# Block attention on row and column tiles: score tiles in pairs, three value buffers, later copies and normalising

## The reference

```python
B, S, D, H = 16, 128, 128, 16          # as called here; a head has D / H = 8 features
q, k, v = split_heads(x @ Wq), split_heads(x @ Wk), split_heads(x @ Wv)
scores = jnp.einsum('bhqd,bhkd->bhqk', q, k) / jnp.sqrt(jnp.float32(HD))
attn_w = jax.nn.softmax(scores, axis=-1)
ctx = jnp.einsum('bhqk,bhkd->bhqd', attn_w, v)
attn_out = ctx.transpose(0, 2, 1, 3).reshape(b, s, d) @ Wo + bo
out1 = _layernorm(x + attn_out, ln1_g, ln1_b)
# then: router on out1, 8 experts, second layernorm
```

## Time and profile before

| | |
|---|---|
| median of 3 runs | 1589.41 us (1586.63 to 1589.45) |
| the profiled execution's own time | 1589.34 us |
| its span, first to last instruction | 1587.6 us |
| outside the span | 1.7 us |
| busy in the span: PE, PEld, DVE, ACT, POOL | 87%, 68%, 53%, 46%, 9% |
| the block attention stage | 1130.1 to 1314.9 us, 184.8 us |
| mean granted TensorE clock | 0.924 of 2.4 GHz |

### The profile page before, as it was taken

One profiled execution on the slowest core, in us unless ns is written; L12 is line 12 of the kernel. 1 busy time (PEld: TensorE's weight loads), 2 busy tenths in 40 slices (PEclk: granted clock), 3 DMA queues, 4 the chain that ended last, 5 costly groups with the idle time before them and its releaser, 6 DMA issues. The chain is left out here.

```text
span 1587.6 us, 27487 instructions
## 1 busy us (share of the span) xinstructions
PE 1382.5 (87%) x9061; PEld 1082.9 (68%) x9061; DVE 839.1 (53%) x2258; ACT 728.7 (46%) x1657; POOL 147.1 (9%) x256
## 2 busy tenths in 40 slices
PE   6765799999996799789999997984699996999995
PEld 5642477777775387579999986973477773666764
DVE  4549676677662554635555543447677762122224
ACT  4331677777762402245555552442355542333333
POOL 1010000000001000000000002005244421000000
PEclk9869899999996999879999997995699996999998
DMA  8000000000000000000000004002000000000000
GB/s 330 1 1 0 1 1 1 2 1 1 1 1 1 1 1 0 1 1 2 1 1 1 1 2 105 16 1 106 0 1 1 0 1 1 1 1 1 0 1 27
DMA packets 6429, 24.55 MB, mean 15 GB/s; under 512 B 797, under 2 KB 1311, under 8 KB 5418
## 3 DMA queue, kind: packets, MB, share of 16 engines
q1 hardware_dynamic: 6314, 23.03, 4.2%
HBM read 21.98 MB, written 1.05 MB: 15 GB/s over the span
## 5 line engine op out<-in xcount | busy, mean ns | idle before, releaser
L1306 DVE SCALAR_TENSOR_TENSOR XN<-bank,gate,XN 128x128 f32<-128x128 f32 x256 | 89.8, 351 | 224.7 <-PE bank L1270 222.2
L1286 ACT ACTIVATE e_hidden<-bank,small 128x512 f32<-128x512 f32 x152 | 104.4, 687 | 214.5 <-PE bank L1258 214.4
L766 PE MATMUL bank<-a_va,a_pT 128*128 128x65 f32 x1024 | 130.3, 270 | 0.7 <-ACT a_pT L933 0.6
L1011 DVE TENSOR_REDUCE a_mx<-bank 128x4 f32<-128x512 f32 x128 | 87.9, 686 | 80.0 <-PE bank L806 79.7
L1270 PEld LDWEIGHTS bank<-attention_weights,e_hidden 128*128 128x128 f32 x1024 | 119.2, 192 | 14.8 <-issue 14.8
L766 PEld LDWEIGHTS bank<-a_va,a_pT 128*128 128x128 f32 x1024 | 125.2, 193 | 2.5 <-ACT a_pT L933 1.1
L1258 PE MATMUL bank<-XNT,attention_weights 128*128 128x512 f32 x256 | 121.2, 606 | 1.2 <-PEq L541 1.2
L1270 PE MATMUL bank<-attention_weights,e_hidden 128*128 128x128 f32 x1024 | 119.3, 275 | 0.0
L831 PE MATMUL bank<-attention_weights,a_cv 128*128 128x256 f32 x256 | 84.4, 411 | 15.0 <-issue 15.0
L933 ACT ACTIVATE a_pT<-bank 128x512 f32<-128x512 f32 x128 | 76.1, 595 | 41.9 <-PE bank L840 39.2
L1019 DVE TENSOR_TENSOR a_shifted<-bank,a_mx 128x512 f32<-128x512 f32 x128 | 88.3, 690 | 3.4
(11 more groups left out here) (351 smaller groups left out, 2709.9 us busy)
## 6 DMA issues: line engine op xcount, KB each, us to landing
attention_weights<-in_a SPq DMA_DIRECT2D x2, 2048.0 KB, 11.8
mod_ring<-in_mod_weights SPq DMA_DIRECT2D x4, 576.0 KB
ctx_both<-in_ctx SPq DMA_DIRECT2D x1, 2048.0 KB, 9.5
attention_weights<-in_up SPq DMA_DIRECT2D x1, 2048.0 KB, 7.7
attention_weights<-in_down SPq DMA_DIRECT2D x1, 2048.0 KB, 13.7
down<-in_down SPq DMA_DIRECT2D x1, 1536.0 KB, 18.3
down<-in_mod_weights SPq DMA_DIRECT2D x2, 576.0 KB
X<-in_x SPq DMA_DIRECT2D x4, 256.0 KB, 3.9
```

Of the source, the lines that this page charges most:

```text
L766: last = pe.matmul(value_bank[:, j * (W + 1):(j + 1) * (W + 1)], pT[:, i.slot(2), j * 128:(j + 1) * 128], va[:, p, g // 2 * 8 + 2 * j + g ...
L1011: dve.tensor_reduce(mx[:, i.slot(2), :], score_bank[i.slot(2)][:, :].rearrange("p (h s) -> p h s", h=4), AX.X, ALU.max).then_inc(maxed, 1)
L1286: act.activation(hidden[0:rows, p, f, :], up_bank_of(i, f)[0:rows, :], function, bias=up_bias(g, f)).then_inc(hidden_ready, 1)
L1306: dve.scalar_tensor_tensor(out=total, in0=down_bank[j][:, e * D:(e + 1) * D], scalar=gate_column(k, 4 * q + j, g * per_group + e), in1=tot ...
```

## The change

**Scores on row tiles.** The projected q and k lie with 4 heads in each group of 32 rows. `kD` shrinks from 16 masked copies of k to 4: copy j keeps in every group of 32 rows the rows of that group's head j (mask `own`, made once on DVE). The scores of group r are a matmul over rows 32r to 32r+31 alone, and the matmuls of two groups follow each other in different row tiles of the array and different banks. There are four score banks in place of two. POOL makes `kD` with one instruction a batch in place of four.

**Values on column tiles.** The roles are swapped: a window of 32 columns of `va` is the weight, the transposed probabilities (128 columns) move, and the result appears already transposed, 32 partitions a group of four heads. A head's 8 features stand in `va` every 40 columns with zeros between, so that a window at 32j past a group's start holds head j at its own place and zeros elsewhere; four matmuls accumulate in a column tile. A second set of 16 matmuls with a weight of ones gives every row its sum. All 32 of a batch are issued together, once `pT` of all four items is kept (`pT` now holds 2 batches of 4 items), and three buffers of `va` take turns. The turn of the result and ACT's copy of it fall away, and DVE's reciprocal covers 128 columns.

**The probabilities' turn** is now an ordinary matmul with the identity as the moving side.

**Later steps.** ACT's copy of `pT` gets a lag of its own, 6. Lags change from NORM_O 6, OUT 7, ADD 7, NORMALISE 8, KEEP 9, TURN_OUT 10 to NORM_O 8, OUT 8, ADD 9, NORMALISE 10, AFFINE 11, KEEP 15, TURN_OUT 15. Scale and shift of the output and its copy go from DVE to POOL (AFFINE). The output's bank half moves: `y_bank` shares the values' bank, the turned output the projection's. PE's order within a step becomes project, values, turn P, score, out, turn out. All sweeps of the stage are written out without a loop.

```diff
-    PROJECT, KEEP_QKV, BLOCKS, SCORE, EXP, TURN_P, VALUES, NORM_O, TURN_O, OUT, ADD, NORMALISE, KEEP, TURN_OUT = \
-        0, 1, 4, 3, 5, 5, 6, 6, 7, 7, 7, 8, 9, 10
+    PROJECT, KEEP_QKV, BLOCKS, SCORE, EXP, TURN_P, KEEP_P, VALUES, NORM_O, OUT, ADD, NORMALISE, AFFINE, KEEP, TURN_OUT = \
+        0, 1, 2, 3, 5, 5, 6, 6, 8, 8, 9, 10, 11, 15, 15
...
+        score_bank, turn_bank, value_bank, project_bank = k.ps[0:4], k.ps[4:6], k.ps[6], k.ps[7]
+        turned_out, y_bank = project_bank[:, 384:512], value_bank[:, 256:384]
...
-            pool.memset(va[:, :, :, W:W + 1], 1.0).then_inc(cleared, 1)
+            pool.memset(va[:, :, :], 0.0).then_inc(cleared, 1)
+            pool.memset(ones[:, :], 0.0).then_inc(cleared, 1)
+            pool.wait_ge(cleared, 2)
+            pool.memset(ones[:, :].rearrange("p (j w) -> p j w", w=40)[:, :, 0:W], 1.0).then_inc(cleared, 1)
...
+                i = at(VALUES)
                 if i.alive and i.offset % 4 == 3:
+                    n, p = b.number, b.slot(2)
+                    await_count(pe, p_kept, 4 * n + 4)
                     if b.older_than(1):
+                        await_count(pe, o_normed, n)
+                        await_count(pe, added, n)
...
+                    for at_column, stationary, per_group in ((0, va[:, n % 3, :], 160), (S, ones[:, :], 0)):
+                        for j in range(4):
+                            for c in range(4):
+                                first = c * per_group + 32 * j
+                                last = pe.matmul(value_bank[32 * c:32 * c + 32, at_column:at_column + S],
+                                                 stationary[:, first:first + 32], pT[:, p, c, j * 128:(j + 1) * 128],
+                                                 start=j == 0, stop=j == 3, tile_position=(0, 32 * c))
...
-                        last = pe.transpose(turn_bank[p][:, j * 128:(j + 1) * 128],
-                                            probs[:, p, j * 128:(j + 1) * 128], k.ident)
+                        last = pe.matmul(turn_bank[p][:, j * 128:(j + 1) * 128],
+                                         probs[:, p, j * 128:(j + 1) * 128], k.ident, start=True, stop=True)
...
+                i = at(SCORE)
+                if i.alive and i.offset % 2 == 0:
+                    await_count(pe, k_spread, b + 1)
+                    if i.older_than(4):
+                        await_count(pe, subtracted, m - 2)
+                    for r in (g, g + 1):
+                        rows = slice(32 * r, 32 * r + 32)
+                        pe.matmul(score_bank[r][:, :], qT[rows, p, :],
+                                  kD[rows, p, :, :].rearrange("p h s -> p (h s)"), start=True,
+                                  stop=True).then_inc(scored, 1)
...
+                i = at(NORM_O)
                 if i.alive and i.offset % 4 == 3:
...
+                    dve.reciprocal(rec[:, :], value_bank[:, S:2 * S]).then_inc(inverted, 1)
...
+                    dve.tensor_tensor(oT[:, :], value_bank[:, 0:S], rec[:, :], ALU.mult).then_inc(o_normed, 1)
...
                 i = at(SCORE)
                 if i.alive:
-                    await_count(dve, scored, m + 1)
+                    await_count(dve, scored, m + 2 - i.offset % 2)
                     dve.tensor_reduce(mx[:, p, :], bank, AX.X, ALU.max).then_inc(maxed, 1)
```

More of the change, by code:

```diff
@@ L1843, in body @@
                 i = at(BLOCKS)
[L1844 to L1852, removed]
+                if i.alive and i.offset % 4 == 0:
+                    b = batch_of(i)
+                    n, p = b.number, b.slot(2)
+                    await_count(pool, qkv_kept, n + 1)
+                    if b.older_than(2):
+                        await_count(pool, scored, 4 * n - 4)
+                    elif n == 0:
+                        pool.wait_ge(own_ready, 1)
+                    pool.tensor_tensor(kD[:, p, :, :], kT[:, p, :].unsqueeze(1).to_broadcast([128, 4, S]),
+                                       own[:, :].unsqueeze(2).to_broadcast([128, 4, S]), ALU.mult).then_inc(k_spread, 1)
+                i = at(AFFINE)
+                if i.alive and i.offset % 4 == 3:
+                    b = batch_of(i)
+                    n, p = b.number, b.slot(2)
+                    await_count(pool, scaled_ready, n + 1)
+                    if b.older_than(2):
+                        await_count(pool, out_turned, n - 1)
+                        await_count(pool, copied, n - 1)
+                    pool.tensor_tensor(out[:, p, :], scaled[:, p, :], k.affine3(2), ALU.mult).then_inc(chain, 1)
+                    await_count(pool, chain, n + 1)
+                    pool.tensor_tensor(out[:, p, :], out[:, p, :], k.affine3(3), ALU.add).then_inc(out_ready, 1)
+                    await_count(pool, out_ready, n + 1)
+                    pool.tensor_copy(col(k.out1, n), out[:, p, :]).then_inc(copied, 1)
+            sweep(pool, G, 8, TURN_OUT, body, rolled=False)
         @block.tensor
@@ L1859, in body @@
             def body(at):
[L1860 to L1864, removed]
                 i = at(PROJECT)
@@ L1875, in body @@
                               stop=True).then_inc(projected, 1)
[L1876 to L1884, removed]
@@ L1916, in body @@
                     b = batch_of(i)
-                    await_count(pe, o_kept, b.number + 1)
-                    pe.matmul(side_bank[:, 128:256], k.ones[0:1, :], k.bias3[0:1, :], start=True, stop=False)
-                    pe.matmul(side_bank[:, 128:256], oT[:, :], k.w3[:, 384:512], start=False,
+                    await_count(pe, o_normed, b.number + 1)
+                    pe.matmul(y_bank, k.ones[0:1, :], k.bias3[0:1, :], start=True, stop=False)
+                    pe.matmul(y_bank, oT[:, :], k.w3[:, 384:512], start=False,
                               stop=True).then_inc(y_done, 1)
-            sweep(pe, G, 8, TURN_OUT, body)
+                i = at(TURN_OUT)
+                if i.alive and i.offset % 4 == 3:
+                    b = batch_of(i)
+                    await_count(pe, out_ready, b.number + 1)
+                    await_count(pe, qkv_kept, min(b.number + 5, B))
+                    if b.older_than(1):
+                        await_count(pe, out_kept, b.number)
+                    pe.transpose(turned_out, out[:, b.slot(2), :], k.ident).then_inc(out_turned, 1)
+            sweep(pe, G, 8, TURN_OUT, body, rolled=False)
         @block.scalar
```

112 lines of the change are left out of this document (51 added, 61 removed).

## The result

The changed kernel takes 1641.3 us (1640.43 to 1642.16, 4 runs) against 1589.43 us (1586.63 to 1590.13, 4 runs) for the kernel before: ratio 1.033, 95% interval 1.0314 to 1.0345, so 51.9 us slower. The forecast was 1672 us, 82 us slower. The profiled execution took 1640.43 us, its span 1638.6.

What follows compares the result with a forecast made beforehand. Took PE to bound the old stage and a ring through all engines the new: start at 1150, 15 intervals of 15.9 us less 1.6, then 3.5 and 6.8, ending 82.3 us later; forecast 1672 us, range 1636 to 1722.

Steps and rivals of the forecast that it cites:

- PE's sum: PE's own work per batch in the block attention: 9.3 us, 1.4 below the 10.7 before.
- a ring through PE, DVE and ACT: Block attention: engines wait for each other in a circle from scores to next scores, 14.3 us a batch at full clock.
- the two places named: PE stands still about 1.5 us before the ring's first turn and 2.5 to 2.9 us before the values.
- the case that had a chance of 0.04: Parts of the chain of waits hidden: 10.8 to 13.5 us a batch, 1593 to 1634 us; chance 0.04.
- signs of being right: Values' interval 14 to 16 us, PE 60 to 75% busy, values waiting for `pT`'s copy, clock below 1.00, reciprocal about 1.0 us.
- half clock: PE's clock falls after a 2.9 us pause in every batch, adding 1.6 us: 15.9 us a batch.
- first values start: First batch's value matmuls in the block attention start at 1150 us, after two rounds of scores of 4.3 us each.
- last interval shorter: The last of the fifteen batch intervals lacks a second pair of scores and is 1.6 us shorter.
- from last values to the end: End of the stage: last values 3.5 us, mostly at half clock, then a tail of 6.8 us.
- Rival 1: Block attention: same 14.3 us a batch, but the clock stays at 2.4 GHz; 1646 us, chance 0.24.
- Rival 2: Values' column tiles don't overlap: values 7.3 us, 19.5 us a batch, 1729 us; chance 0.13, shared with clock low throughout.
- Rival 3: PE remains the bound at 9.3 us a batch since DVE and ACT run ahead; 1571 us, chance 0.05.

## Why the prediction was right, and where it was off

The direction and the mechanism were right: PE's sum fell, a ring through PE, DVE and ACT took its place as the bound, and PE waits at the two places named. The size was 82 us where 52 were measured.

That the time lies in the wide range (1636 to 1722) is in part luck. It lies 5 us above the lower end and outside the forecast's own range (1655 to 1690). The interval at full clock, 13.31 us, is in the case that had a chance of 0.04 and that the range left out (10.8 to 13.5 us a batch, 1593 to 1634), and among the signs of being right the interval of 14 to 16 us failed. By the forecast's own sum 13.31 us with the clock up gives 1631; the 7.0 us of half clock in four batches and a start 3.1 us late bring the time into the range. With the pause filled, the same ring took 1635.7. The other signs held: PE busy 74.6% in the windows above, the clock at 0.95, the `pT` copy 0.1 us from the end of the Exp, the values' 64 records in 1.9 us and the reciprocal at 0.947.

By the terms of its own sum, counted from the values' starts:

| term | forecast, us | measured, us | difference |
|---|---|---|---|
| first values start | 1150 | 1153.12 | +3.1 |
| ring, 15 intervals at full clock | 15 x 14.3 | 15 x 13.31 | -14.9 |
| half clock | 15 x 1.6 = 24 | 204.93 - (15 x 13.31 - 1.76) = 7.0 | -17.0 |
| last interval shorter | 1.6 | 1.76 | -0.2 |
| from last values to the end | 10.3 | 1366.48 - 1358.05 = 8.4 | -1.9 |

The 1.76 is 13.31 less the last interval of the kernel with six more matmuls (11.55). The differences add up to -30.9 us, which takes the stage's end from the forecast 1397.2 to 1366.3; it was at 1366.48.

**The clock.** This term was mis-sized most, by 17 us. The prediction had the clock fall in every batch, from one pause of 2 us elsewhere. It fell in 4 of 16. A fall cost 1.4 to 1.7 us in the steady part, as forecast (at the last interval 14.06 - 11.55 = 2.5); how often it came was wrong. Rival 1, with the clock up throughout, gave 1646, and the kernel with the pause filled took 1635.7: so the rival's condition was nearer, while its ring was as long as the forecast's.

**The ring's steps**, counted from the scores' start (1237.21), forecast and measured: next pair 4.5 and 4.55; scaling done 6.05 and 5.46; the add of x 8.85 and 8.41; Ln 9.9 and 9.27; `pT` copy 10.5 and 9.70; values 11.2 and 10.34; next turn 13.25 and 12.22; next scores 14.3 and 13.31 (the last two from batches at full clock). Up to the second pair the sum is right to 0.05, though by errors that cancel: from the scores to the maximum 1.20 for 1.06, from there over the normalising to the subtraction 0.86 for 1.07, from the turn to the next pair 1.09 for 0.99. Then 0.3 us go because the scaling was taken to end behind the scores' arrival, while it ended before, as the run with a narrow reciprocal in this kernel confirms: the path goes through the scores. The remaining 0.7 lies in the values (1.9 for 2.05) and in small overlaps. The rows of durations that I summed are longer than the steps from start to start: DVE's 0.69 us steps start 0.61 to 0.73 apart, Ln, Exp and copy (0.29, 0.20, 0.58) start 0.33 and 0.10 apart, and the copy's successor 0.48 after it.

**PE's work.** Column tiles overlap fully: the 64 records of values and sums fill 1.9 us (1234.24 until the turns at 1236.12), with the change of kind, against 2.05 forecast and an estimated 7.0 in series (64 records of 0.11). The Trainium skill (TensorE: Matmul & The Clock Gate, Measured speedup vs the span model) gives 2.38 times for three column tiles, from which the prediction estimated 2.9 us. The trace has 1.9, an estimated 7.0 / 1.9 = 3.7 times for four tiles, so it is better than what that figure gives. Rival 2 fell with it, and the pairs of scores overlap as the earlier trace rows had it: a pair takes 1.06 us until the next kind, for 1.1. The turns came out dearer, 4.0 us a batch for 3.6 (0.12 to 0.126 a record for 0.11), which with the rest makes 9.57 for 9.3. One row was misread for the kernel before: 25.6 us of idle loads in 140 are 2.0 us a batch, not 0.5. The 0.5 was only what the sum of 10.2 lacked to 10.7, and nothing in the forecast rests on it.

**Rival 3** (faster, PE stays the bound, 1571 us) was wrong for this kernel by its order alone: with both lists changed the same operations took 1574.28. Its condition, a ring below PE's own sum, was the right one.

**Start and end.** The first values came 3.1 us late, again by errors that partly cancel. The first scores started at 1134.95 for 1137.5. The two rings of the start took 6.29 us each (1134.95, 1141.24, 1147.53) for 4.3, since they ran wholly at half clock, where the prediction had that for the scores only, and 5.6 us followed for 3.4. The end was 1.9 shorter, 1.6 of it because the last values, taken at half clock in the forecast, ran at the full one.

## What to carry over

When a change takes work off the bounding engine, follow one round through all engines' lists before believing the gain; here a pair of score matmuls behind the values and a 0.5 us root ahead of a copy turned a gain of 14.5 us (21 forecast) into a loss of 52, and moving two blocks gave it back. That an engine's instructions stand back to back (DVE at 97%) doesn't make it the bound; an experiment that shortens one of them tells. Steps from start to start, not durations, are to be summed along a chain.

## What the runs showed of the hardware

- Of the pauses ahead of the 16 batches' values, 2.4 us in the steady part with the same work around them, four (the last of them 3.0 us long) were followed by half clock and the rest were not. Filled up to 1.1 us by six small matmuls, none was. So a pause of this length has no fixed price.
- Taking 16 records a batch off PE made the ring 0.9 us shorter and the program no faster (1643.8 against 1641.3 us): its granted clock over 1150 to 1350 us was 0.75 in place of 0.95.
- The 64 records of 32 matmuls on four column tiles, 128 columns each, start 0.028 us apart (0.90 us for 32 records), a quarter of the 0.11 of records in series.
- The reciprocal of 128x128 took 0.947 us, of 128x16 0.25 us, where other DVE operations of 128x128 take 0.28 to 0.35.
